# A graph network's gathers: 806 tiles without holes in place of 840, sums held node by row, and a deeper sort

## The reference, cut to what matters

```python
for l in range(3):
    X = einsum('ne,ref->rnf', out, weights[l])
    msg = X[edge_type, src] + biases[l][edge_type]
    hidden = segment_sum(msg, dest, num_segments=N)
    out = relu(hidden) if l < 2 else hidden
x = layernorm(x + out)
...
alpha = beta * cos(x[row], x[col])
out = segment_sum(softmax_over_row(alpha) * x[col], row)
x = layernorm(x + out)
```

## Time and profile before

| | |
|---|---|
| median of 3 runs | 4264.41 us (4263.59 to 4267.21) |
| the profiled execution: its time, and its span | 4270.03 us, 4268.3 us |
| busy, share of the span: PE, PEld, DVE, ACT, POOL | 73%, 43%, 57%, 20%, 64% |
| mean granted clock of PE, share of full speed | 0.862 |

### The profile page before, as it was taken

The page is one execution under the profiler, slowest core; times in us unless marked ns, Lnnn a source line. Parts: engine busy times, 40 slices in busy tenths (PEclk is TensorE's granted clock), DMA queues, the critical chain, the costliest instruction groups (busy, mean ns, idle before and its releaser), DMA issues.

```text
span 4268.3 us, 55641 instructions
## 1 busy us (share of the span) xinstructions
PE 3096.6 (73%) x13925; PEld 1821.7 (43%) x13926; DVE 2434.5 (57%) x9103; ACT 857.6 (20%) x1992; POOL 2752.9 (64%) x2839
## 2 busy tenths in 40 slices
PE   7799957676776678667667667777775655656998
PEld 4455424333433334333334333344333434434776
DVE  9888855554555556555554554465554333335999
ACT  2599801001001000001001001001000000002665
POOL 0777777777777772777777777647777777772000
PEclk9899979999899997999998998898997555556999
DMA  4100013333433437333333333553433222224564
GB/s 157 42 2 2 2 45 83 78 71 80 80 72 78 81 72 175 70 72 76 83 72 74 84 74 71 71 175 76 83 72 85 53 53 53 53 53 76 185 192 141
DMA packets 377130, 343.02 MB, mean 80 GB/s; under 512 B 263666, under 2 KB 327722, under 8 KB 376712
## 3 DMA queue, kind: packets, MB, share of 16 engines
q0 software_dynamic: 90368, 165.49, 19.7%
q1 hardware_dynamic: 83112, 113.25, 8.0%
q10 hardware_dynamic: 203360, 60.73, 5.9%
HBM read 232.12 MB, written 107.13 MB: 79 GB/s over the span
## 4 chain that ended last, share of the span: by engine, by line
POOL 63%; issue 21%; PE 9%; DVE 5%; DMA 2%; ACT 1%; SPq 0%; POOLq 0%; DVEq 0%; ACTq 0%
POOL region L817 55%; POOL scattered_edges L800 8%; PE ps L958 2%; PE ps L929 2%; PE ps L986 2%; DMA region<-x_of_type,arrays 1%; DVE region L340 1%; DVE region L608 1%; PE ps L961 1%; PE ps L919 1%; DVE region L580 0%; PE ps L908 0%; DVE arrays L368 0%; DVE arrays L379 0%; DVE region L599 0%
## 5 line engine op out<-in xcount | busy, mean ns | idle before, releaser
L817 POOL DMA_INDIRECT region<-x_of_type,arrays x2520 | 2415.7, 959 | 918.9 <-issue 764.9
L908 PE MATMUL ps<-oh,region 128*128 128x102 f32 x5040 | 1261.3, 340 | 725.9 <-DMA region<-x_of_type,arrays 707.0
L441 DVE TENSOR_SCALAR oh<-iota_w,arrays 128x102 f32<-128x102 f32 x2528 | 724.3, 290 | 1703.7 <-PE ps L908 1701.4
L919 PE MATMUL ps<-region 128*128 128x510 f16 x4200 | 1402.0, 410 | 346.8 <-issue 195.8
L908 PEld LDWEIGHTS ps<-oh,region 128*128 128x128 f32 x5040 | 1000.1, 228 | 1454.9 <-DMA region<-x_of_type,arrays 1281.2
L919 PEld LDWEIGHTS ps<-region 128*128 128x128 f16 x4200 | 434.5, 113 | 549.8 <-issue 527.2
L505 DVE TENSOR_TENSOR region<-region,ps 128x102 f32 x2520 | 646.1, 256 | 3.6 <-issue 3.2
L1048 ACT COPY region<-ps 128x510 f32<-128x510 f32 x155 | 89.8, 579 | 2482.8 <-PE ps L919 2482.3
L800 POOL DMA_INDIRECT scattered_edges<-region x304 | 332.8, 1095 | 207.0 <-DVE ends L398 109.3
L887 PE MATMUL ps<-region 128*128 128x420 f16 x2016 | 362.6, 342 | 24.9 <-ACT region L1025 24.9
L1025 ACT ACTIVATE region<-region 128x128 f16<-128x128 f16 x1008 | 348.8, 394 | 39.7 <-DVE region L418 29.6
(11 more groups left out here) (173 smaller groups left out, 1486.4 us busy)
## 6 DMA issues: line engine op xcount, KB each, us to landing
region<-x_of_type,arrays POOLq DMA_INDIRECT x2520, 2.6
edge_counts<-region ACTq DMA_DIRECT2D x155, 255.0 KB
arrays<-edge_counts SPq DMA_DIRECT2D x40, 960.0 KB, 5.0
x_of_type<-region SPq DMA_DIRECT2D x50, 576.0 KB, 3.9
edge_absent<-region ACTq DMA_DIRECT2D x155, 127.5 KB
region<-edge_absent SPq DMA_DIRECT2D x40, 480.0 KB, 4.4
x_of_type<-x0st SPq DMA_DIRECT2D x51, 192.0 KB, 1.8
scattered_edges<-region POOLq DMA_INDIRECT x304
```

Source lines behind the costliest of these rows:

```text
L441: ins = nc_.tensor_scalar(oh[:, t % U, 0:RB], iota_r, rowf[:, t % NT:t % NT + 1], None, ALU.is_equal)
L817: pool.indirect_dma_start(out=grow[:, t % GR, :], out_offset=None, in_=xt, in_offset=bass.IndirectOffsetOnAxis(ap=gix[:, t:t + 1], axis=0) ...
L908: mm = pe.matmul(ps[:, 6 + n % 2, t * RB:(t + 1) * RB], grow[:, u % GR, :], oh[:, u % U, 0:RB], start=True, stop=True)
L919: mm = pe.matmul(ps[:, c, 0:CW], cl[:, q % CR, c * P:(c + 1) * P], cr[:, q % CR, :], start=False, stop=False, skip_group_check=True)
```

## The change

- **No holes.** Edges of one group follow the last group's at once: 103125 edges fill `GT` = 806 tiles. A tile that holds edges of two groups is used once for each of them. So PE and DVE still go through 840 places in a layer (`NT`), but POOL gathers 806 tiles, into `GR` = 62 places. Which gathered tile a place uses, and where it lies in `grow`, are read into PE's registers (`slots_at` for 8 places at once, `tile_due` for 4 at once). One-hots are masked by the row: an edge of another group has a row outside 0 to 101.
- **One semaphore for the gathers.** SP waits for the gathers one by one and passes each on (`pass_on`, `s_seq`); PE waits once per 4 tiles, for the last that they need.
- **The product the other way round.** The one-hot (102 columns) is loaded as weights and the gathered tile (128 columns) moves; the sums lie node by row in `hn` (102 partitions, 31 x 128 columns). Behind each layer PE turns the 31 blocks and DVE takes them out of PSUM, with relu or without (`turn_sums`, `take_turned`).
- **Rings.** Three banks of sums for two, twelve one-hots for eight, 8 places for the counts' one-hots for 5.
- **The sort.** `KR` = 28 places, and `s_put` once per `KS` = 14 columns. The tables for the registers are made on DVE between its columns (`plan`).
- **The gather index** now takes a turn: since a place is no longer a tile, the words are turned on PE (7 transposes), copied by ACT, and moved by a product with shifted one-hots (`pick`, 8 matmuls), before DVE writes `gix`.

The diff, cut to its core (constants that stay, names of semaphores and buffers are left out):

```diff
-GR = 24
+GR = 62
+PAIRS = 8
+SUMS = 3
+OH = 12
-KR = 4
+KR = 28
+KS = 14
...
+    GT = -(-E // P)
+    LAP = MB - 1
+    ROUNDS = GT // GR
...
-            step(nc_.tensor_scalar(tot, tot, float(P - 1), None, ALU.add))
-            step(nc_.tensor_copy(smi[:, 0, :], tot))
-            step(nc_.tensor_scalar(smi[:, 1, :], smi[:, 0, :], 7, None, ALU.arith_shift_right))
-            step(nc_.tensor_copy(til, smi[:, 1, :]))
+            step(nc_.tensor_tensor_scan(til, tot, tot, 0.0, ALU.add, ALU.bypass))
+            nc_.tensor_scalar(smi[:, 1, :], til, float(P - 1), None, ALU.add)
+            step(nc_.tensor_tensor(smi[:, 0, :], til, tot, ALU.subtract))
...
             for t in range(EP):
                 k = t % KR
                 q, c = (cols[:, 4 * t + n:4 * t + n + 1] for n in range(2))
-                if t >= KR:
-                    dve.wait_ge(s_put, t - KR + 1)
+                if t >= KR and t % KS == 0:
+                    dve.wait_ge(s_put, (t - KR) // KS + 1)
                 nc_.tensor_scalar(hot_q[:, k, :], iota_s[:, 0:P], q, None, ALU.is_equal).then_inc(s_hot, 1)
                 nc_.tensor_scalar(oh_s[:, k, :], iota_s, c, None, ALU.is_equal).then_inc(s_cell, 1)
+                if t % 8 == 4 and t // 8 in MIDWAY:
+                    plan(MIDWAY.index(t // 8))
...
-            step(nc_.tensor_tensor(wide[:, 0:NT], wide[:, 0:NT], w, ALU.add))
-            step(nc_.tensor_scalar(g, wide[:, 0:NT], -1.0, None, ALU.add))
+            step(nc_.tensor_tensor(w, wide[:, 0:NT], w, ALU.add))
+            step(nc_.tensor_scalar(v, w, (1 << ROW_BIT) - 1, None, ALU.bitwise_and))
+            step(nc_.tensor_copy(wide[:, 0:NT], v), "words")
+            step(nc_.tensor_scalar(g, w, -1.0, None, ALU.add))
             step(nc_.tensor_scalar(v, g, ROW_BIT, None, ALU.arith_shift_right))
-            nc_.tensor_copy(rowf[:, 0:NT], v)
-            step(nc_.tensor_scalar(g, g, (1 << ROW_BIT) - 1, None, ALU.bitwise_and))
-            step(nc_.tensor_scalar(g, g, float(R * NP - 1), None, ALU.min))
-            nc_.tensor_copy(rowf[:, NT:KW], rowf[:, 0:GR])
-            step(nc_.tensor_copy(gix[:, NT:KW], gix[:, 0:GR]), "rows")
+            step(nc_.tensor_copy(rowf[:, 0:NT], v))
+            dve.wait_ge(s_pt, 1)
+            nc_.tensor_scalar(gix[:, 0:512], ps[:, 4, 0:512], -1.0, 0.0, ALU.add, ALU.max)
+            step(nc_.tensor_scalar(gix[:, 512:GT], ps[:, 5, 0:GT - 512], -1.0, 0.0, ALU.add, ALU.max), "rows")
...
-                    dve.wait_ge(s_add, i * BODY + (first + u + 2 * SLOTS))
-                    h = hA[:, bass.ds(bs[t], RB)]
-                    nc_.tensor_tensor(h, h, ps[:, 6 + n % 2, t * RB:(t + 1) * RB], ALU.add).then_inc(s_add, 1)
+                    dve.wait_ge(s_add, i * BODY + (first + u + SUMS * SLOTS))
+                    h = hn[0:RB, bass.ds(bs[t], D)]
+                    nc_.tensor_tensor(h, h, ps[0:RB, 5 + n % SUMS, t * D:(t + 1) * D], ALU.add).then_inc(s_add, 1)
+
+            def take_turned(l, n, relu):
+                lo, hi = SLOTS * n * RB, min(SLOTS * n + SLOTS, MB) * RB
+                dve.wait_ge(s_tn, HN * (l - 1) + n + 1)
+                if relu:
+                    nc_.tensor_scalar(hB[:, lo:hi], ps[:, 5 + n % XB, 0:hi - lo], 0.0, None, ALU.max).then_inc(s_feat, 1)
...
+            def pass_on(l):
+                for t in range(GT):
+                    sp.wait_ge(s_g[t % GR], 16 * (ROUNDS * l + t // GR + 1))
+                    sp.sem_inc(s_seq, 1)
...
-                for t in range(NT):
-                    n = NT * l + t
-                    if t % SLOTS == 0 and n >= GR:
-                        pool.wait_ge(s_used, n // SLOTS - RINGS + 1)
+                for t in range(GT):
+                    last = t + SLOTS - 1 - GR + LAP
+                    if t % SLOTS == 0 and t + SLOTS - 1 >= GR:
+                        pool.wait_ge(s_used, NT // SLOTS * l + last // SLOTS + 1)
...
-                    pe.wait_ge(s_g[u % GR], i * (16 * BODY // GR) + 16 * ((first + u) // GR + 1))
+                    if u % PAIRS == 0:
+                        at = slots_at((i * BODY + u) // PAIRS)
+                        due = values_of(pe, tile_due, (i * BODY + u) // PAIRS, GT, PAIRS // SLOTS, 1)
                     if t == 0:
+                        reg_wait(pe, s_seq, due[u % PAIRS // SLOTS] + GT * l)
                         pe.wait_ge(s_oh, i * (BODY // SLOTS) + (first // SLOTS + n + 1))
                         pe.wait_ge(s_add, i * BODY + (first + u + SLOTS))
-                    mm = pe.matmul(ps[:, 6 + n % 2, t * RB:(t + 1) * RB], grow[:, u % GR, :], oh[:, u % U, 0:RB],
+                    mm = pe.matmul(ps[0:RB, 5 + n % SUMS, t * D:(t + 1) * D], ohr[:, u % OH, 0:RB], grow[:, bass.ds(at[u % PAIRS], D)],
                                    start=True, stop=True)
...
-                        if c % 2 == 0:
-                            reg_wait(pe, s_cz, ready + min(c + 1, CG - 1))
+                            reg_wait(pe, s_cz, ready[q % CL] + (CG - 1))
...
+            def turn_sums(l):
+                pe.wait_ge(s_add, NT * l + SUMS * SLOTS)
+                for n in range(HN):
+                    if n >= XB:
+                        pe.wait_ge(s_feat, HN * (l - 1) + n - XB + 1)
+                    for t in range(min(SLOTS, MB - SLOTS * n)):
+                        b = SLOTS * n + t
+                        mm = pe.transpose(ps[:, 5 + n % XB, t * RB:(t + 1) * RB], hn[0:RB, b * D:(b + 1) * D],
+                                          ident[0:RB, 0:RB])
+                    mm.then_inc(s_tn, 1)
+                pe.wait_ge(s_feat, HN * l)
```

More of the change, by code:

```diff
@@ L61, in gnn_program @@
     TURNS = NT // BODY
-    KW = NT + GR
-    RINGS = GR // SLOTS
+    KW = NT + BODY
+    GT = -(-E // P)
+    LAP = MB - 1
+    ROUNDS = GT // GR
+    assert GT + LAP <= NT and ROUNDS * GR == GT and GR >= LAP + BODY and NT % PAIRS == 0 and PAIRS % SLOTS == 0
+    SLOT_SHIFT = 16
+    SLOT_MUL = -(-(1 << SLOT_SHIFT) // GR)
+    assert GT * SLOT_MUL < 1 << 24 and all(t * SLOT_MUL >> SLOT_SHIFT == t // GR for t in range(GT))
+    HN = -(-MB // SLOTS)
+    TC = -(-NT // P)
+    PW = P + 32
+    SLO = [max(0, P * c - 32) for c in range(TC)]
+    SHI = [min(GT, P * c + P) for c in range(TC)]
+    assert LAP <= 32
     CP = 304
@@ L175, in gnn_program @@
         iota_s = part(NT // 2, F16)
-        used[0] = NK * ET // 2
+        used[0] = MB * D
         cols = part(EP * 4)
@@ L181, in gnn_program @@
         hot_q = part(KR * P // 2, F16).rearrange("p (u q) -> p u q", u=KR)
+        pick = part(TC * PW).rearrange("p (c g) -> p c g", c=TC)
+        wordt = part(TC * P)
         assert used[0] <= NK * ET
@@ L200, in gnn_program @@
         unit = part(NP).rearrange("p (b d) -> p b d", b=NB)
-        used[0] = max(GR * D, NP) + NP
+        hA = part(NP)
         ring = part(RING * SC).rearrange("p (u w) -> p u w", u=RING)
@@ L283, in sums_at, with slots_at @@
             return nc.values_load_multi_w_load_instructions(
-                blkt[0:1, bass.ds(k * SLOTS, SLOTS)], engines=[mybir.EngineType.DVE], min_val=0, max_val=(MB - 1) * RB,
-                skip_runtime_bounds_check_because="blkt holds RB times a group from 0 to MB - 1, made in this program")[1]
+                blkt[0:1, bass.ds(k * SLOTS, SLOTS)], engines=[mybir.EngineType.DVE], min_val=0, max_val=(MB - 1) * D,
+                skip_runtime_bounds_check_because="blkt holds D times a group from 0 to MB - 1, made in this program")[1]
+        def slots_at(k):
+            return nc.values_load_multi_w_load_instructions(
+                slot_at[0:1, bass.ds(k * PAIRS, PAIRS)], engines=[mybir.EngineType.PE], min_val=0, max_val=(GR - 1) * D,
+                skip_runtime_bounds_check_because="slot_at holds D times a tile's number modulo GR, made in this program")[1]
         def reg_wait(eng, s, value):
@@ L413, in _ @@
+            MIDWAY = range(8, 8 + 2 * (13 + TC), 2)
             for t in range(EP):
@@ L529, in _ @@
                         take_tiles(l, i, False)
+            for n in range(HN):
+                take_turned(L, n, False)
             def moments(z, b):
@@ L864, in _ @@
             for n in range(2):
-                mm = pe.matmul(ps[:, 5 + n, 0:HW], ones[0:MB - 1, :], past_t[0:MB - 1, n * HW:(n + 1) * HW],
+                pe.matmul(ps[:, 5 + n, 0:HW], ones[0:MB - 1, :], past_t[0:MB - 1, n * HW:(n + 1) * HW],
+                          start=True, stop=True)
+            for n in range(2):
+                pe.matmul(ps[:, 4 + 3 * n, 0:HW], shiftw[0:MB - 1, :], past_t[0:MB - 1, n * HW:(n + 1) * HW],
+                          start=True, stop=True)
+            for c in range(TC):
+                w = min(P, NT - P * c)
+                mm = pe.matmul(ps[0:w, 4, HW + c:HW + c + 1], past_t[0:MB - 1, P * c:P * c + w], shiftcol[0:MB - 1, 0:1],
                                start=True, stop=True)
@@ L941, in _ @@
             pe.wait_ge(s_cz, CG + CG * MB)
[L942 to L943 removed]
+            turn_sums(L)
```

(12 more changed lines are left out.)

172 lines of the change are left out of this document (128 added, 44 removed).

## The result

Measured: 4211.32 us (median of 4 runs, 4209.0 to 4221.98) against 4264.88 us in the same session. The ratio is 0.9879, 95% interval 0.9861 to 0.9896. The change is faster by 1.2%, 54 us where 133 were forecast, and the time lies above the range of 4104 to 4180.

The account below looks back on a forecast made before the run. POOL, issuing gathers and waiting for nobody, was taken to bound the kernel. The terms -128.8 - 13 + 22 + 5.5 - 19 = -133.3 us, taken from 4264.4, gave 4131 us; range 4104 to 4180.

Parts of the forecast that it names:

- Fewer gathers: In the three layers, 34 fewer gathers each, at POOL's unchanged pace of 1.268, 1.264 and 1.257 us: -128.8 us.
- The end of a layer: From POOL's last gather to the layer's last addition, 11.7, 11.7 and 8.1 us: -13 us, bounds -25 and -3.
- The turn: Behind each layer, 31 turns and 8 moves stand before the next matmuls: +22 us, bounds +13 and +25.
- Table, sort and first gather: Before the layers: longer index preparation +5.5 us; sort's scatters at 1.32 us for 1.43, -19 us.
- A: In the sort, trains of DVE instructions starve POOL's scatters, slower: 4331 us; chance 0.03.
- B: PE bounds the layers, its clock kept at 1.2 GHz by waiting in lumps: +240 us, 4370; chance 0.04.
- C: In the layers, places and not gathers set the pace, 1.26 us each; no change, 4260 us; chance 0.03.
- D: PE's pauses at group changes or a slower sort give back 30 to 80 us: 4165 to 4215; chance 0.12.
- E: In the layers, a faster gather pace as well: under 4105 us; chance 0.05.

Follow-up runs that it names:

- a_hot102: The changed kernel with product and addition over 128 rows, one-hots still written over 102 columns, the other 26 cleared once: 4110.31 us (kernel before 4264.56).
- h2_timed: The kernel of a_hot102 timed again with repeats in a later session: 4117.85 us against 4272.1 for the kernel before, ratio 0.9639.
- b_lump: The kernel before, with PE waiting for the gathers of four tiles at once: 4267.22 us (kernel before 4274.19).
- a_p128: The changed kernel with one-hots, product and addition all over 128 rows: 4114.24 us (kernel before 4274.19).
- a_hot128: The changed kernel with only the one-hots over 128 columns, product and addition staying on 102 rows: 4218.7 us (kernel before 4264.56).
- b_add102: The kernel before, with its addition on partitions 0 to 101 alone: 4357.21 us (kernel before 4264.56).
- b_cl102: The kernel before, with only the counts' 640-column one-hot made on 102 partitions: 4325.87 us (kernel before 4277.63).
- b_all102: The kernel before, with all DVE instructions of the layers' loop, but for the first eight one-hots, on 102 partitions: 4271.24 us against 4271.05.

## Why the prediction was wrong, step by step

**Fewer gathers: the step that failed.** "-128.8 us, if POOL keeps its pace." It did not: 1.320, 1.308 and 1.277 us per gather for 1.268, 1.264 and 1.257. The term measured -36. The change turned the product round, and the prediction asked only what that costs PE; that the addition thereby goes from 128 to 102 partitions, among one-hots on 128, was never costed, on the very port for which the prediction had shown holds. With product and addition on 128 (a_hot102), the three layers are 139 us shorter than before, more than the forecast, since the hold even falls from 37 to 25 us. PE kept up, as argued: POOL never waited for it longer than the 0.3 us that lie between two gathers anyway.

**The end of a layer.** -13 forecast. From POOL's last gather to the last addition: 1611.80 - 1600.17 = 11.6, then 10.7 and 7.7 us, together -14. Right, to 1 us in each layer; the last gather lands 2.6 to 2.7 us after its start, 1.7 after POOL's end, where 2.5 were said.

**The turn.** +22 forecast, between +13 and +25. The turn keeps the next matmuls back until 4.6, 4.6 and 5.4 us after the last addition, where these were 0.6, 0.6 and 0.2: +13. The bound came out. The forecast let PE's turns set the pace, at 0.204 us each; 31 of them took 3.68 us behind the first two layers, 0.12 each, and the 8 moves of DVE beside them, 3.9 us, set it. The timeline behind the second layer:

```profile
2734.09 3.68 PE L1075 MATMUL ps<-ident,region 102*128 102x102 f32 x31 [2.03 <-DVE region L602]
2734.70 3.90 DVE L608 TENSOR_SCALAR hB<-ps 128x408 f32<-128x408 f32 x8 [0.66 <-PE ps L1075]
...
2738.65 3.82 PE L1086 MATMUL ps<-wsb,hB 128*128 128x384 f32 x11 [0.88 <-DVE hB L608]
```

Another 6 us, not forecast, went from what follows. Of these 4.5 lie in the 150 instructions of L929, now L1086: 51.45 and 50.34 us at a granted clock of 0.94 and 0.97 before, 48.68 and 48.64 at 1.00 after. Time times clock is 48.4 and 48.8 before, so the clock can be all of it; no run tests that.

**Table, sort and first gather.** -19 and +5.5, together -13.5; measured -17.3. From the addition of the two tables to the first gather pass 9.7 us (527.05 to 536.76) for 4.6, +5.1 where +5.5 were forecast; that addition starts 22.4 us earlier, where 19 were forecast and 22 was the bound. The hold of most scatters did vanish: 242 of the last 259 take less than 0.99 us, for 25 before, and free ones step at 1.26 us. The table is now there before the sort ends (scatters done at 510 us), so that the sort itself, 362 us as before, and 12 us of preparation set the first gather. DVE's wait of 20.7 us went entirely. The estimate of 1.32 us per scatter measured 1.295.

**The sum without the failed step.** The span of a_hot102 is 4108.6, 154 us under the kernel before of its session (4262.8), where 133 were forecast and -160 was the end of the bounds; the repeated runs (h2_timed) give 154 as well. In its layers the same -129 became -139, beside a profile whose span was 5.5 us longer than in that session. So without the failed step the forecast of 4131 would have been 13 to 21 us too high (4110.31 and 4117.85 us), inside the range.

**The rivals.** *A* named the right resource and the wrong place: not the scatters in the sort, which got faster, but the gathers in the layers; and not longer trains alone, as b_lump shows, though in the changed kernel a gather is indeed held over two or three DVE instructions in a row. The rule of the Trainium skill (SBUF — State Buffer, "Who interferes with whom") has DVE, in its two-port modes, keep GpSimd from a shared port for the whole of an instruction; the rows of the kernel before agree (0.81 us behind the end of that instruction). In the changed kernel it is two or three for 194 of the 533 held gathers, which goes beyond what the rule says. *B*: the clock in the layers did fall, 0.92 to 0.83 and 0.84, as in b_lump, and bounded nothing: POOL waited for nobody. *C*, places set the pace, is refuted by a_hot102: 806 gathers take 1017 us there at 1.262 us each, over the same 840 places. *D* covers the number, 4165 to 4215, but by pauses of PE or a slower sort, and neither came; that the time fell into its span is luck. *E*, under 4105, did not come, neither here nor with the addition on 128.

**What is shown and what is not.** Shown: the addition on fewer partitions makes the holds (a_hot102 against a_p128 and a_hot128, b_add102); another kind of instruction does so too (b_cl102); equal counts don't (b_all102). Open: why the alternation makes a gather wait for a second instruction, even between two of 128 partitions that follow each other, and behind additions, and whether it is so with other pairs of counts than 128 with 102 or 96. Nor is alternation the only way to it: beside four casts in a row, all on 128 partitions, the scatter of 2.36 us of the earlier trace rows was held over more than one instruction in the kernel before.

## What to carry to other kernels

When the chain lies on an engine that waits for nobody, look at its own durations: a shorter list is worth its length only if one entry costs what it did. Price each change of shape on a neighbour that can hold that engine as if it lay on the path, and here keep the partition count of DVE's instructions the same throughout a loop beside GpSimd's indirect DMAs, even at the price of rows that nobody reads. Give unused places of a gather distinct rows.

## What was not expected of the hardware

- 102 and 128 partitions alternating on DVE lengthen POOL's gathers from 959 to 995 ns on average (b_add102), 2% of the whole time, without DVE itself taking longer. With 102 throughout, they take 960 ns.
- Gathers whose 128 descriptors name one row land 10 to 14 us after their issue; with distinct rows 2.5 to 4.1 us.
- A steady rhythm on DVE can catch POOL's: with one signal per column (and 4 places) scatters step at 1.43 us on average, which is two columns of the sort; with one per 14 (and 28 places) at 1.29 to 1.30. In the changed kernel with 4 places it is 1.405.
- A session in which the same kernel takes 5139 us for 4272, with engines that stand still for nothing in the program.
